# Out-degrees counted as a 128 by 49 table instead of 64 by 98, and seven tiles' row statistics moved from ScalarE to VectorE

## What is computed

```python
h_hc  = layernorm(x)                       # 6250 x 256
m     = clifford_linear(h_hc[src] * r_hc[edge_type], msg_w, msg_b)
m     = m * sigmoid(gate(r))
deg_src = segment_sum(ones, src)           # how often each node is a source
deg_dst = segment_sum(ones, dst)
m     = m * maximum(deg_src[src] * deg_dst[dst], 1) ** -0.5
x     = x + clifford_linear(h_hc + segment_sum(m, dst), upd_w, upd_b)
# experts: for each of 8: relu(bn(x W1)), relu(bn(h W2)), h Wo, weighted by a softmax router
x     = x + sum_e w_e * expert_e(layernorm(x))
```

## Time and profile before

| | |
|---|---|
| median of 3 runs | 2031.54 us (2031.03 to 2038.73) |
| the profiled execution | 2032.06 us |
| its span, first to last instruction | 2030.2 us |
| TensorE busy | 1940.5 us, 96% of the span |
| VectorE, ScalarE, GpSimd busy | 897.1, 678.7, 1398.8 us |
| mean granted TensorE clock | 0.948 |

### The profile page before, as it was taken

The page is one execution under the profiler, slowest core; times in us unless marked ns, Lnnn a source line. Parts: engine busy times, 40 slices in busy tenths (PEclk is TensorE's granted clock), DMA queues, the critical chain, the costliest instruction groups (busy, mean ns, idle before and its releaser), DMA issues.

```text
span 2030.2 us, 34715 instructions
## 1 busy us (share of the span) xinstructions
PE 1940.5 (96%) x13129; PEld 1766.1 (87%) x13130; DVE 897.1 (44%) x2024; ACT 678.7 (33%) x1384; POOL 1398.8 (69%) x1402
## 2 busy tenths in 40 slices
PE   5993998999999999999999999999999999999998
PEld 5992887888899899889989989988998998898888
DVE  4555544344444444444444444444444444444342
ACT  2802232233323323333333333333233233333445
POOL 3822777777777777777777777777777777777600
PEclk8555898999999999999999999999999999999999
DMA  7216543443444344344344434434434443444300
GB/s 235 82 29 198 184 120 105 122 121 99 125 121 122 106 122 119 104 125 122 104 125 120 120 104 121 121 104 123 122 107 119 123 120 104 121 120 113 88 12 6
DMA packets 96806, 231.47 MB, mean 114 GB/s; under 512 B 24617, under 2 KB 45351, under 8 KB 96729
## 3 DMA queue, kind: packets, MB, share of 16 engines
q0 software_dynamic: 65856, 182.73, 32.8%
q1 hardware_dynamic: 30058, 46.73, 7.2%
q10 hardware_dynamic: 815, 1.16, 0.2%
HBM read 217.08 MB, written 13.44 MB: 114 GB/s over the span
## 4 chain that ended last, share of the span: by engine, by line
PE 84%; POOL 9%; issue 3%; DMA 1%; DVE 1%; ACT 1%; SPq 0%; POOLq 0%; DVEq 0%
PE z L693 31%; PE y L723 16%; PE agg L738 15%; PE pr L747 8%; PE y L618 7%; POOL H L386 6%; PE y L669 3%; POOL R L386 3%; PE y L660 2%; PE z L645 1%; PE y L681 1%; PE y L661 1%; DMA H<-h_table,src 1%; DMA h_table<-big 1%; PE y L715 0%
## 5 line engine op out<-in xcount | busy, mean ns | idle before, releaser
L386 POOL DMA_INDIRECT H<-h_table,src x784 | 785.1, 1001 | 309.3 <-issue 235.4
L386 POOL DMA_INDIRECT R<-r_table,typ x588 | 601.7, 1023 | 202.5 <-issue 202.5
L548 ACT ACTIVATE h<-z,bns 128x256 f32<-128x256 f32 (+1 forms) x864 | 416.7, 539 | 903.1 <-PE z L693 900.7
L1069 DVE SCALAR_TENSOR_TENSOR acc<-y,wg,acc 128x256 f32<-128x256 f32 x392 | 173.4, 480 | 575.2 <-PE y L723 575.1
L738 PE MATMUL agg<-S,H 128*86 128x64 f32 x4704 | 397.9, 243 | 0.0
L738 PEld LDWEIGHTS agg<-S,H 128*86 128x86 f32 x4704 | 393.9, 160 | 0.1
L693 PE MATMUL z<-hT,big 128*128 128x256 f32 (+1 forms) x1728 | 386.3, 368 | 2.2 <-ACT h L548 2.2
L723 PE MATMUL y<-big,h 128*128 128x256 f32 x1568 | 378.2, 382 | 1.7 <-DVE lg L1032 1.6
L693 PE MATMUL z<-h,big 128*128 128x256 f32 (+1 forms) x1728 | 376.6, 361 | 0.4
L693 PEld LDWEIGHTS z<-h,big 128*128 128x128 f32 x1728 | 306.6, 192 | 36.2 <-ACT h L548 1.0
L723 PEld LDWEIGHTS y<-big,h 128*128 128x128 f32 x1568 | 292.0, 190 | 41.5 <-issue 1.9
(11 more groups left out here) (163 smaller groups left out, 990.9 us busy)
## 6 DMA issues: line engine op xcount, KB each, us to landing
H<-h_table,src POOLq DMA_INDIRECT x784, 2.8
tb<-in_typ_row SPq DMA_DIRECT2D x25, 448.0 KB
R<-r_table,typ POOLq DMA_INDIRECT x588, 2.8
h_table<-big SPq DMA_DIRECT2D x7, 910.0 KB, 8.3
big<-in_x SPq DMA_DIRECT2D x7, 896.0 KB, 10.9
big<-in_w SPq DMA_DIRECT2D x8, 768.0 KB, 4.4
acc<-in_x SPq DMA_DIRECT2D x22, 256.0 KB, 3.8
out<-acc SPq DMA_DIRECT2D x22, 256.0 KB
```

Source lines behind the costliest of these rows:

```text
L386: pool.indirect_dma_start(out=ring[:, slot, b * DX:(b + 1) * DX], out_offset=None, in_=tab, in_offset=bass.IndirectOffsetOnAxis(ap=ix[:, J ...
L548: last = s_.activation(o[:, m, 0:wide_], z_[:, m, 0:wide_], ACT.Relu, bias=bns[:, l, 1, c:c + 1], scale=bns[:, l, 0, c:c + 1])
L1069: last = v.scalar_tensor_tensor(out=acc[:, g % 3, t, :], in0=b[:, t * D:(t + 1) * D], scalar=wg[:, t, e_:e_ + 1], in1=acc[:, g % 3, t, :], ...
```

## The change

The index is split 128 by 49 instead of 64 by 98 (`P - 1` and a shift by 7 in place of `LO - 1` and 6). The stationary one-hot now has 128 columns, the moving one 49, and PSUM holds the degrees as 128 by 49 at once, so that the copy at line 889 and the two folding matmuls go, with two GpSimd instructions that made a shifted identity. VectorE's loop is cut in two, and between the halves, behind 16 of the 28 groups, VectorE takes the mean and variance of the last seven tiles (`bn_stats`, `bn_aggr`), while ScalarE does 42 tiles (XS = 42) and waits for `x_stats` before its root. The one-hot buffers, the integer table (3584 columns instead of 2744) and the destination indices move in SBUF.

```diff
+    XS = NT - XN if XC > 1 else NT
-    LO, HI = 64, 2 * NT
-        oh_lo = [part(HB * LO // 2)...
-        oh_hi = [part(HB * HI // 2)...
+        oh_lo = [part(HB * P // 2)...
+        oh_hi = [part((HB * NT + 1) // 2)...
+        dst_i = Rflat[:, 4 * D:4 * D + NB].bitcast(i32)
-        ps_bins = Yp[0:LO, 0, 0:HI]
-        ps_deg = Yp[:, 0, 256:256 + NT]
+        ps_deg = Yp[:, 0, 0:NT]
...
-                for c in range(1, XC):
+                for c in range(1, XS // XN):
                     sums_of(c)
-                for t in range(NT):
+                for t in range(XS):
                     link(s_.activation(sq, xall[:, t, 0:D], ACT.Square, bias=mean[:, t:t + 1],
                                        accum_out=ssq[:, t:t + 1]))
                 act.wait_ge(consts, 2)
+                act.wait_ge(x_stats, 1)
...
-                            last = pe.matmul(ps_bins, oh_lo[h][:, :, b], oh_hi[h][:, :, b],
+                            last = pe.matmul(ps_deg, oh_lo[h][:, :, b], oh_hi[h][:, :, b],
                                              start=False, stop=True, skip_group_check=True)
                         last.then_inc(oh_used, 1)
                 pe.wait_ge(consts, 2)
-                pe.wait_ge(deg_bins, 1)
-                pe.matmul(ps_deg, ident[0:LO, :], deg_lo[:, 0:HI:2], start=True, stop=False)
-                pe.matmul(ps_deg, half, deg_lo[:, 1:HI:2], start=False, stop=True).then_inc(deg_mm, 1)
...
-                            for oh, part_, m in ((oh_hi[h], hi_b, HI), (oh_lo[h], lo_b, LO)):
+                            for oh, part_, m in ((oh_hi[h], hi_b, NT), (oh_lo[h], lo_b, P)):
...
-                onehots(first, HIT)
-
-                dve.wait_ge(oh_used, 2 + 2 * HIT)
-                v.tensor_copy(deg_lo, ps_bins).then_inc(deg_bins, 1)
+                onehots(first, (first + HIT) // 2)
+                if XS < NT:
+                    dve.wait_ge(ld_x[XC - 1], 16)
+                    for t in range(XN):
+                        last = v.bn_stats(xst[:, t, :], xall[:, XS + t, 0:D])
+                    link(last)
+                    for t in range(XN):
+                        last = v.bn_aggr(xmv[:, t, :], xst[:, t, :])
+                    link(last)
+                    v.tensor_scalar(mean[:, XS:NT], xmv[:, :, 0:1].rearrange("p t o -> p (t o)"), -1.0, None, ALU.mult)
+                    v.tensor_scalar(ssq[:, XS:NT], xmv[:, :, 1:2].rearrange("p t o -> p (t o)"), float(D), None, ALU.mult).then_inc(x_stats, 1)
+                else:
+                    dve.sem_inc(x_stats, 1)
+                onehots((first + HIT) // 2, HIT)
+
                 dve.wait_ge(ln_sd, 1)
                 v.reciprocal(rstd[:, :], rstd[:, :]).then_inc(nm_in, 1)
-                dve.wait_ge(deg_mm, 1)
+                dve.wait_ge(oh_used, 2 + 2 * HIT)
                 v.tensor_scalar(dsr, ps_deg, 1.0, None, ALU.max).then_inc(ds_in, 1)
```

More of the change, by code:

```diff
@@ L64, in build @@
     RT = nrel // 4
+    XC = 7 if NT % 7 == 0 else 1
+    XN = NT // XC
+    XD = (4 * XN + 6) // 7
+    XS = NT - XN if XC > 1 else NT
     T = 2 * P
     HB = max(h for h in range(1, 29) if NB % (2 * h) == 0)
-    LO, HI = 64, 2 * NT
-    IC = max(LO, HI)
     ds = bass.ds
@@ L160, in part @@
             return hflat[:, at[0] - words:at[0]]
[L162 to L166, removed]
+        oh_lo = [part(HB * P // 2).bitcast(bf16).rearrange("p (c b) -> p c b", b=HB) for i in range(2)]
+        iota_cb = part(HB * P // 2).bitcast(bf16).rearrange("p (c b) -> p c b", b=HB)
+        oh_hi = [part((HB * NT + 1) // 2).bitcast(bf16)[:, 0:HB * NT].rearrange("p (c b) -> p c b", b=HB) for i in range(2)]
+        dst_i = Rflat[:, 4 * D:4 * D + NB].bitcast(i32)
         lo_b = S[:, :, :, :].rearrange("p a b c -> p (a b c)")[:, 0:NB // 2].bitcast(bf16)
@@ L170, in build @@
         hi_i = hflat[:, NB:2 * NB].bitcast(i32)
-        assert 2 * NB <= oh_at + HB * HI // 2
+        assert 2 * NB <= HB * P
         rext = part(4 * DX).rearrange("p (k c) -> p k c", k=4)
@@ L178, in build @@
         ones0 = h2flat[0:1, 3 * D:3 * D + P]
-        half = hgB[0:LO, 0, 0:P]
-        deg_lo = hgB[0:LO, 0, P:P + HI]
         bo4 = carry[0:4 * NE, 1, 0, :]
@@ L190, in build @@
         sq = hgA[:, 0, :]
+        xst = hgB[:, 0, 0:6 * XN].rearrange("p (t c) -> p t c", c=6)
+        xmv = hgB[:, 0, 6 * XN:8 * XN].rearrange("p (t c) -> p t c", c=2)
         gbc = gwb[:, D:D + 1]
@@ L199, in build @@
         Yp = ctx.enter_context(nc.psum_tensor("y", [P, 2, 512], fp32))
-        ps_bins = Yp[0:LO, 0, 0:HI]
-        ps_deg = Yp[:, 0, 256:256 + NT]
+        ps_deg = Yp[:, 0, 0:NT]
         ps_base = Yp[:, 1, 0:NSB]
         ps_flag = Yp[0:1, 1, 256:256 + P]
-        XC = 7 if NT % 7 == 0 else 1
-        XN = NT // XC
-        XD = (4 * XN + 6) // 7
         HIT = NB // (2 * HB)
@@ L218, in build @@
         w2_zero, zeroed, dd_in, row_ready = (sem(x) for x in ("w2_column", "sums_zeroed", "dd_in", "row_ready"))
+        x_stats = sem("x_stats")
         nm_in, nm_ready = sem("nm_in"), sem("nm_ready")
-        deg_bins, deg_mm = sem("deg_bins"), sem("deg_mm")
         tb_ld = [sem(f"types_loaded{i}") for i in range(3)]
@@ L357, in _ @@
                 pool.memset(ones0, 1.0)
-                pool.memset(half, 0.0)
                 pool.memset(ident[:, :], 0.0).then_inc(pool_own, 1)
@@ L364, in _ @@
                 pool.wait_ge(pool_own, 3)
-                pool.affine_select(out=half, in_=half, compare_op=ALU.not_equal, fill=1.0,
-                                   base=LO, pattern=[[-1, P]], channel_multiplier=1)
                 pool.affine_select(out=ident[:, :], in_=ident[:, :], compare_op=ALU.not_equal, fill=1.0,
@@ L462, in _ @@
                 act.dma_start(rtab[nrel:nrel + 1, :], zrow).then_inc(tab_r, 16)
-                for c in range(1, XC):
+                for c in range(1, XS // XN):
                     sums_of(c)
-                s_.activation(mean[:, :], ssum, ACT.Copy, scale=-1.0 / D).then_inc(stats, 1)
+                s_.activation(mean[:, 0:XS], ssum[:, 0:XS], ACT.Copy, scale=-1.0 / D).then_inc(stats, 1)
                 act.wait_ge(stats, 1)
-                for t in range(NT):
+                for t in range(XS):
                     link(s_.activation(sq, xall[:, t, 0:D], ACT.Square, bias=mean[:, t:t + 1],
@@ L852, in link @@
                     dve.wait_ge(z_dve, count[0])
-                v.memset(ps_bins, 0.0).then_inc(oh_done, 1)
+                v.memset(ps_deg, 0.0).then_inc(oh_done, 1)
                 dve.wait_ge(iotas, 1)
-                v.tensor_copy(iota_cb, iota_w[:, 0:IC].unsqueeze(2).to_broadcast([P, IC, HB]))
+                v.tensor_copy(iota_cb, iota_w[:, 0:P].unsqueeze(2).to_broadcast([P, P, HB]))
                 dve.wait_ge(ld_src, 16)
-                v.tensor_scalar(lo_i, src[:, :], LO - 1, None, ALU.bitwise_and)
-                link(v.tensor_scalar(hi_i, src[:, :], 6, None, ALU.logical_shift_right))
+                v.tensor_scalar(lo_i, src[:, :], P - 1, None, ALU.bitwise_and)
+                link(v.tensor_scalar(hi_i, src[:, :], 7, None, ALU.logical_shift_right))
                 v.tensor_copy(lo_b, lo_i)
```

## The result

| | before | changed |
|---|---|---|
| median of 4 runs | 2034.13 us | 1986.80 us (1986.29 to 1990.45) |
| ratio, 95% interval | | 0.9769 [0.9744, 0.9795] |
| the profiled execution | 2032.06 us | 1986.29 us |
| TensorE starts the degrees | 26.19 | 27.16 |
| the degrees are read (line 893, now 896) | 162.40 | 110.72 |

The kernel is 2.3% faster. The degrees are read 51.7 us earlier (54.2 forecast), the first H gather is 45.7 us earlier (49.2 forecast), and the profiled execution ends 45.8 us earlier.

A forecast was written before the change was run, and what follows sets the result against it. The degree matmuls (134.69 us, paced by TensorE) were taken to hold back the first H gather. With h_table landing at 137.5 against 186.70, 2032.06 less 49.2 gave 1982.9, forecast 1982 us, range 1974 to 2008.

The forecast's parts named there:

- What bounds: Start of the kernel: degree matmuls delay the first H gather; the end moves with that gather, 49 us earlier.
- The moving stream: Degree matmuls: 49 moving columns at 1.75 ns each set the pace, 86 ns a matmul, 2.40 us a group.
- the round trip: Degree loop, TensorE and VectorE through two buffers: 5.55 us for two groups, 2.78 us a group.
- The stationary stream: Degree matmuls: loading 128 stationary columns instead of 64 takes 86 to 120 ns; 86 taken.
- line 747's 120 ns: Line 747 loads 128 packed columns per pass, passes 0.12 us apart at full clock: at most 120 ns a load.
- rival 1: Degree matmuls: the strided stationary load becomes the bound at 224 ns a matmul, end at 2071 us; chance 0.17.
- the subtraction of rests: Line 618's load record less a rest of 81 to 125 ns: 72 to 116 ns for 64 stationary columns.
- VectorE and the statistics: Degree loop: a comparison pair costs 2.72 us instead of 2.50; the moved statistics add 3.8 us, not hidden.
- ScalarE: Statistics before the degrees: seven sums and squares fewer save 8.2 us, root at 85.8, holding nobody.
- GpSimd: R gathers beside comparisons: one per 2.78 us period, 22 during comparisons, 3 during statistics, the last 20 ending at 130.
- Rival 3: R gathers: none passes during back-to-back comparisons, GpSimd becomes the bound, end at 2003 us; chance 0.08.
- Storing: Storing h_table: 24.3 us plus 5 for R gathers sharing the DMA engines, bounds 0 and 7; lands at 137.5.

The follow-up runs named there:

- The run with ten superblocks: Changed kernel with R gathers of 10 superblocks instead of 15 ahead of the H gathers, on another chip: 2421.11 us, ratio 0.9869.

## Why the prediction was right

**What bounds.** Right. The end of the profiled execution moved by 45.8 us and the first H gather by 45.7, 49.2 forecast. The 3.5 us between are 2.5 in the read of the degrees and 1.0 in the storing, both below. GpSimd issues 1327 gathers behind the first H gather with hardly a wait, and its stretch of issuing is as long as before (1731.6 and 1731.8 us), so what the start gained came through whole. That TensorE is as full there leaves open which of the two engines sets that length.

**The moving stream,** 86 ns forecast, and the matmul is paced at 91 ns at full clock and 93 at half. The price of 1.75 ns a column was nearly right: beside the packed load 49 columns passed in 87 ns. That the load of 128 hides without a rest was not: it adds some 4 ns. The clock, which I left out, is worth another 1 to 2. The 7 ns together lengthen the round trip: two groups take 5.77 us (41.57 to 47.34) where I had 5.55, and over all 26 groups it is 2.85 us each, against 2.78.

**The stationary stream.** The value came out nearly right, and my reason for it was wrong. I took line 747's 120 ns as the nearest row because it too has 128 columns. But those are packed, and the runs show that packed or not makes a factor of two, and that 127 columns at this stride cost 240 ns. The rows could not decide between 86 ns and rival 1, whose strided price is what 127 columns really pay (224 forecast, 240 measured). As far as the rows go, the choice was luck. What speaks for it is the rule that stood beside it (the Trainium skill, TensorE: Matmul & The Clock Gate, section Weight-path perf modes — Fast Weight Load (FWL) and DoubleRow). The runs agree with it in both of its conditions that they touch: 128 columns get the fast load and 127 and 64 don't, and a stride is allowed. The page's factor of about two is here at least 240/93 = 2.6, as the moving stream has a part in the 93. That the load was hidden in the kernel before was right (64 columns cost 123 ns, the pace was 172), but the subtraction of rests that I used gave 72 to 116 ns for it, too little.

**VectorE and the statistics.** 2.72 us a pair forecast, 2.74 measured (64.67 to 67.41). 3.8 us for the statistics, 3.33 measured. On the path, as forecast; not covered, as forecast. TensorE's later start (27.16 instead of 26.19; GpSimd's signs are ready 0.5 us later, and the six matmuls end another 0.5 behind them) adds 1.0 us, 26 groups at 0.07 us more add 1.8, and the shorter statistics take 0.5 back. These are 2.3 of the 2.5 us by which the read comes later than the 108.2 forecast.

**ScalarE.** Root at 86.76 us, 85.8 forecast; it then waited 23.9 us.

**GpSimd.** One gather a group, 26 by the end of the comparisons (25 forecast), the last one at 132.5 (130). The warning of the Trainium skill (GPSIMD Engine Reference, section Key points) holds: gathers of 2.4 to 2.7 us beside comparisons with two SBUF inputs, 0.95 without. Rival 3 did not come.

**Storing.** From the read to the first H gather 31.1 us against 25.0, 6.0 more, 5 forecast for the sharing. The run with ten superblocks shows 4.1 of this on another chip, where the changed kernel took 29.7. The other runs whose R gathers reach as far into the storing took 29.6, 29.6 and 31.4, so the rest is within what this distance varies by.

**Not seen at all:** VectorE's small instructions that crawl beside gathers on some chips. They did not touch the first result, where the first matmul of line 747 (now 739) moved by 52 us, from 195.3 to 143.5. On the other chips it moved by 40 (195.6, read in the kernel before with the statistics moved, to 155.5).

## What to carry to other kernels

A one-hot table can be split so that the side with exactly 128 columns is the stationary one: 128 by 49 was faster than 64 by 98, and its degree part also than that of 64 by 49. A reading of the nearest row is only as good as what the row shares with the case: here the count and the stride both mattered, and two runs with 127 columns told it. And when a wait goes, look at what used to run alone in the time behind it: the R gathers slid into the storing and took 4 to 6 us back, and the work that was moved to unload ScalarE landed on the engine that had become the bound.

## What the runs showed of the hardware that I had not expected

- Strided by 56 bytes, the slow stationary load costs 1.89 to 1.93 ns a column (240 ns for 127, 123 ns for 64); packed it costs 0.85 at half the clock (108 ns for 127), and at full clock the pace was 87 ns. With the fast one of 128 strided columns the pace is 91 to 93 ns.
- With 128 stationary and 49 moving columns, both strided, the pace is 91 ns at full clock and 93 at half. With 98 moving columns it is 172 to 174 ns, at either clock.
- The same kernel takes 2034 us on one chip and 2436 to 2464 on three others, with the degree part equal within 1 us.
- On two of those chips a 0.07 us memset of VectorE took 0.7 us while gathers were in flight.
